# Gather indices of a four-layer graph network: one load of 14 groups into half of a 28-group buffer, in place of one load per group

## What is computed

```python
edge_index = jnp.stack([src, dst])
x = _layernorm(x + _L0_gnn_ref(x, edge_index, edge_weight, ...))   # segment_sum(x[src] * edge_weight, dst)
x = _layernorm(x + _L1_gnn_ref(x, edge_index, edge_attr_64, ...))  # segment_sum(relu(x[src] + edge_attr), dst)
x = _layernorm(x + _L2_gnn_ref(x, edge_index, ...))                # segment_sum(x[src], dst), batch norm
x = _layernorm(x + _L3_gnn_ref(x, edge_index, edge_type_8, ...))   # attention over 8 relations, (x @ W[r])[src]
```

## Time and profile before

| | us |
|---|---|
| median of 3 runs (lowest, highest) | 12603.83 (12548.62, 12606.76) |
| the profiled execution | 12571.97 |
| its span on the core | 12570.2 |
| POOL busy in the span | 6491.1 (52%) |
| PE, DVE, ACT busy | 3621.9 (29%), 3237.4 (26%), 329.6 (3%) |
| pass 0 gathers from, to | 11.4, 2535.4 |
| pass 3 gathers from, to | 8331.9, 10916.5 |

### The profile page before, as it was taken

One profiled execution on the slowest core, in us unless ns is written; L12 is line 12 of the kernel. 1 busy time (PEld: TensorE's weight loads), 2 busy tenths in 40 slices (PEclk: granted clock), 3 DMA queues, 4 the chain that ended last, 5 costly groups with the idle time before them and its releaser, 6 DMA issues.

```text
span 12570.2 us, 99249 instructions
## 1 busy us (share of the span) xinstructions
PE 3621.9 (29%) x17244; PEld 2968.1 (24%) x17245; DVE 3237.4 (26%) x5805; ACT 329.6 (3%) x648; POOL 6491.1 (52%) x6716
## 2 busy tenths in 40 slices
PE   2222222242222222432232223640000000003558
PEld 2222222242222222322222222220000000002555
DVE  2111211141111111221111111322222222286554
ACT  0000000010000000000000000100000000000000
POOL 6666666525556566346666665035555555402443
PEclk6555555555555555555555555555555555556885
DMA  1111111111111111111111111232222222302220
GB/s 41 21 21 21 20 21 21 20 37 40 40 41 41 41 42 41 37 27 22 22 22 22 22 22 23 65 100 64 64 65 65 64 66 66 64 0 48 72 71 19
DMA packets 620736, 509.88 MB, mean 41 GB/s; under 512 B 405721, under 2 KB 405721, under 8 KB 620574
## 3 DMA queue, kind: packets, MB, share of 16 engines
q0 software_dynamic: 200704, 212.34, 9.2%
q1 hardware_dynamic: 391778, 239.40, 7.5%
q10 hardware_dynamic: 28224, 57.82, 1.2%
HBM read 405.06 MB, written 103.99 MB: 40 GB/s over the span
## 4 chain that ended last, share of the span: by engine, by line
another core or an unknown queue 32%; issue 21%; DVE 16%; DVEq 15%; PE 14%; ACT 1%; DMA 1%; POOL 0%; ACTq 0%; POOLq 0%; SPq 0%; PEldq 0%
PE p_sum L679 6%; DVEq L213 5%; DVE oh L931 3%; DVEq L931 2%; DVE oh L945 2%; DVEq L926 1%; DVEq L209 1%; PE p_a L777 1%; DVEq L1193 1%; DVEq L1189 1%; DVE sel L1196 1%; DVE sel L1200 1%; DVE msg L1005 1%; PE p_sum L834 1%
## 5 line engine op out<-in xcount | busy, mean ns | idle before, releaser
L486 POOL DMA_INDIRECT gat<-x_d,idx x3136 | 3034.9, 968 | 2241.3 <-DMA idx<-in_src_p 1272.4
L679 PE MATMUL p_sum<-oh,msg 128*66 128x128 f32 (+1 forms) x6272 | 1410.8, 418 | 3681.1 <-DVE oh L931 1676.8
L486 POOL DMA_INDIRECT gat<-rel_d,idx x1568 | 1492.0, 952 | 1612.6 <-DMA idx<-key_d 1079.3
L679 PEld LDWEIGHTS p_sum<-oh,msg 128*66 128x66 f32 (+1 forms) x6272 | 1269.7, 227 | 3821.7 <-DVE oh L931 2910.5
L486 POOL DMA_INDIRECT gat<-in_x,idx x1568 | 1532.4, 977 | 1001.8 <-DMA idx<-in_src_p 526.5
L937 DVE TENSOR_TENSOR sum_t<-sum_t,p_sum 64x128 f32 (+1 forms) x588 | 165.0, 281 | 5204.9 <-remote 4100.1
L679 PE MATMUL p_sum<-oh,gat 128*64 128x128 f32 x3136 | 687.5, 410 | 1723.1 <-DVE oh L931 1184.6
L679 PEld LDWEIGHTS p_sum<-oh,gat 128*64 128x64 f32 x3136 | 616.6, 219 | 1793.8 <-DVE oh L931 1219.6
L931 DVE SCALAR_TENSOR_TENSOR oh<-dstf,fine_col,iota 128x512 f32<-128x512 f32 x1176 | 835.0, 748 | 510.2 <-issue 406.1
L793 PE MATMUL p_sum<-trip_s,oht 128*128 x2344 | 202.0, 237 | 2410.9 <-DVE oht L1193 1255.6
L793 PEld LDWEIGHTS p_sum<-trip_s,oht 128*128 128x128 bf16 x2344 | 168.8, 166 | 2445.6 <-issue 2445.6
(11 more groups left out here) (240 smaller groups left out, 3061.1 us busy)
## 6 DMA issues: line engine op xcount, KB each, us to landing
he_d<-gat ACTq DMA_DIRECT2D x196, 288.0 KB
gat<-he_d SPq DMA_DIRECT2D x196, 288.0 KB, 2.8
ea<-in_edge_attr SPq DMA_DIRECT2D x196, 256.0 KB
gat<-x_d,idx POOLq DMA_INDIRECT x3136
drow<-dst_d SPq DMA_DIRECT2D x196, 256.0 KB
rel_d<-sum_t SPq DMA_DIRECT2D x14, 2016.0 KB, 6.4
gat<-in_x,idx POOLq DMA_INDIRECT x1568
gat<-rel_d,idx POOLq DMA_INDIRECT x1568
```

Of the source, the lines that this page charges most:

```text
L486: nc.gpsimd.indirect_dma_start(out=gat[:, q, s, 0:width], out_offset=None, in_=table, in_offset=bass.IndirectOffsetOnAxis(ap=idx[:, q, s:s ...
L679: ins = nc.tensor.matmul(p_sum[0:width, 0, 0:W], lhs(q, s), oh[:, 0, s, :], start=(s == 0), stop=(s == S - 1))
```

## The change

The index tile gets IB = 28 places in two halves of 14 groups. One load of 14 groups' indices (128 x 112 int32, 56 KB) takes the place of 14 loads of 4 KB. The four data slots, the 8 gathers per group and all that consumes them stay as they are. Loops of SP and POOL that had 49 turns of 4 groups have IL = 7 turns of 28 groups. POOL waits for `s_idx` once in 14 groups, and for `s_free` at every group as before. SP refills a half when its last four groups' slots are freed; in pass 1 it does so between its `ea` loads, in pass 3 after every 14th `dst_row`.

```diff
+HALF = 14
+IB = 2 * HALF
+IL = G // IB
+PER = IB // Q
...
-        idx = sb("idx", [P, Q, S], i32)
+        idx = sb("idx", [P, IB, S], i32)
...
-            def refill(n, q, it, source):
-
-                wait_reg(sp, s_free[q], it + (2 + IT * n))
-                sp.dma_start(idx[:, q, :], source[:, bass.ds(it * Q + (Q + q), 1), :]
-                             .rearrange("p a s -> p (a s)")).then_inc(s_idx[q], 16)
+            def freed(n, it, i):
+
+                wait_reg(sp, s_free[i % Q], it * PER + (i // Q + 2 + IT * n))
+
+            def refill(n, it, h, source, waited=False):
+
+                last = (h + 1) * HALF - 1
+                for i in range(last - Q + 1, last + 1):
+                    if not waited:
+                        freed(n, it, i)
+                sp.dma_start(idx[:, h * HALF:(h + 1) * HALF, :],
+                             source[:, bass.ds(it * IB + (IB + h * HALF), HALF), :]).then_inc(s_idx[h], 16)
...
             def pass3(it, final):
-                for q in range(Q):
-                    if not (final and q >= Q - 2):
-                        wait_reg(sp, s_drused, it * Q + (q + 1))
-                        dst_row(q % 2, it * Q + (q + 2))
-                    if not final:
-                        refill(3, q, it, key_d)
+                for i in range(IB - 2 if final else IB):
+                    wait_reg(sp, s_drused, it * IB + (i + 1))
+                    dst_row(i % 2, it * IB + (i + 2))
+                    if not final and i % HALF == HALF - 1:
+                        refill(3, it, i // HALF, key_d)
...
             def gather_pass(n, table, width):
-                with pool.Fori(0, IT) as it:
-                    for q in range(Q):
-                        wait_reg(pool, s_idx[q], it * 16 + 16 * (1 + IT * n))
-                        wait_reg(pool, s_free[q], it + (1 + IT * n))
+                with pool.Fori(0, IL) as it:
+                    for i in range(IB):
+                        q = i % Q
+                        if i % HALF == 0:
+                            wait_reg(pool, s_idx[i // HALF], it * 16 + 16 * (1 + IL * n))
+                        wait_reg(pool, s_free[q], it * PER + (i // Q + 1 + IT * n))
                         for s in range(S):
                             nc.gpsimd.indirect_dma_start(
                                 out=gat[:, q, s, 0:width], out_offset=None, in_=table,
-                                in_offset=bass.IndirectOffsetOnAxis(ap=idx[:, q, s:s + 1], axis=0),
+                                in_offset=bass.IndirectOffsetOnAxis(ap=idx[:, i, s:s + 1], axis=0),
```

More of the change, by code:

```diff
@@ L141, in program @@
         s_key, s_keyst, s_zero = sem("s_key"), sem("s_keyst"), sem("s_zero")
-        s_idx = [sem(f"s_idx{q}") for q in range(Q)]
+        s_idx = [sem(f"s_idx{h}") for h in range(2)]
         s_gat = [sem(f"s_gat{q}") for q in range(Q)]
@@ L266, in _ @@
             sp.dma_start(edge_w[:, 0:G, :].rearrange(flat), weight_p.rearrange(flat)).then_inc(s_load[2], 16)
-            for q in range(Q):
-                sp.dma_start(idx[:, q, :], src_p[:, q, :]).then_inc(s_idx[q], 16)
+            for h in range(2):
+                sp.dma_start(idx[:, h * HALF:(h + 1) * HALF, :], src_p[:, h * HALF:(h + 1) * HALF, :])\
+                    .then_inc(s_idx[h], 16)
             sp.dma_start(src_i, src_p.rearrange(flat)).then_inc(s_load[3], 16)
@@ L291, in first_indices @@
                     sp.wait_ge(s_free[q], IT * n + 1)
-                    sp.dma_start(idx[:, q, :], source[:, q, :]).then_inc(s_idx[q], 16)
+                for h in range(2):
+                    sp.dma_start(idx[:, h * HALF:(h + 1) * HALF, :], source[:, h * HALF:(h + 1) * HALF, :])\
+                        .then_inc(s_idx[h], 16)
             def dense_io(n):
@@ L364, in dense_io @@
                 sp.sem_inc(s_table, 1)
-            with sp.Fori(0, IT - 1) as it:
-                for q in range(Q):
-                    refill(0, q, it, src_p)
+            with sp.Fori(0, IL - 1) as it:
+                for h in range(2):
+                    refill(0, it, h, src_p)
             sp.wait_ge(s_keyst, 32)
@@ L377, in _, with pass1 @@
                 sp.dma_start(ea_slot[q], ea_d[q, :, :]).then_inc(s_ea[q], 16)
[L378 to L382, removed]
+            def pass1(it, final):
+                for i in range(IB - Q if final else IB):
+                    freed(1, it, i)
+                    sp.dma_start(ea_slot[i % Q], ea_d[bass.ds(it * IB + (Q + i), 1), :, :]
+                                 .rearrange("a p e -> (a p) e")).then_inc(s_ea[i % Q], 16)
+                    if not final and i % HALF == HALF - 1:
+                        refill(1, it, i // HALF, src_p, waited=True)
+            with sp.Fori(0, IL - 1) as it:
+                pass1(it, False)
+            pass1(IL - 1, True)
             dense_io(1)
             first_indices(2, src_p)
-            with sp.Fori(0, IT - 1) as it:
-                for q in range(Q):
-                    refill(2, q, it, src_p)
+            with sp.Fori(0, IL - 1) as it:
+                for h in range(2):
+                    refill(2, it, h, src_p)
             dense_io(2)
@@ L404, in pass3 @@
             def pass3(it, final):
-                for q in range(Q):
-                    if not (final and q >= Q - 2):
-                        wait_reg(sp, s_drused, it * Q + (q + 1))
-                        dst_row(q % 2, it * Q + (q + 2))
-                    if not final:
-                        refill(3, q, it, key_d)
-            with sp.Fori(0, IT - 1) as it:
+                for i in range(IB - 2 if final else IB):
+                    wait_reg(sp, s_drused, it * IB + (i + 1))
+                    dst_row(i % 2, it * IB + (i + 2))
+                    if not final and i % HALF == HALF - 1:
+                        refill(3, it, i // HALF, key_d)
+            with sp.Fori(0, IL - 1) as it:
                 pass3(it, False)
-            pass3(IT - 1, True)
+            pass3(IL - 1, True)
             sp.wait_ge(s_trip, 2)
```

## The result

| | before | after |
|---|---|---|
| median of 4 runs, us | 12597.92 | 12873.42 |
| lowest, highest | 12548.62, 12606.76 | 12866.36, 12892.37 |
| the profiled execution | 12571.97 | 12866.36 |

What follows compares the result with a forecast made beforehand. Bound: POOL's gathers and its pauses, with long bursts starving DVE. 12,572 - 200 (passes 0 to 2) + 390 (pass 3) + 0 (code) = 12,762, plus 32 for the median: 12,790 us, slower by 1.5%; range 12,180 to 13,140.

Steps and rivals of the forecast that it cites:

- What bounds the kernel: Four gather passes: POOL gathers or waits; a long burst of gathers starves DVE, freed some 4 us after POOL pauses.
- Passes 0 to 2: -200: Index load leaves 189 pauses, 1.9 us each, 360 us if nothing else moves; 200 us saved taken, ends 0 and 360.
- the share that DVE takes back: Passes 0 to 2: DVE loses the free time POOL gains; something over half of 360 us kept as saving, unmeasured.
- The sign to look for: Passes 0 to 2: no POOL wait ends with indices; pauses 2 us shorter in the middle, 7.1 in pass 0.
- Pass 3: +390: Pass 3: index waits no longer brake POOL, bursts of 14 groups starve DVE; 390 us longer, 2,996 us.
- The period of 14 groups: Pass 3: 140 us burst, DVE at rate 0.25 after 13 us, then 67, 4 and 3 us: 214 in place of 186.
- to this come 4 us until DVE moves: Pass 3, each pause after a 14-group burst: DVE moves again 4 us after POOL stops.
- About 13 long waits of 70 us: Sign in pass 3: POOL gathers 140 us without pause, then waits some 70 us for indices, about 13 times, not 61.
- DVE's waits in pass 3: Sign in pass 3: DVE's waits by "remote" and "issue" grow.
- Loops' code: 0: POOL's longer loop body, 28 turns: code fetches of 76 to 306 us possible, taken as zero, hidden in pauses.
- DVE keeps up: Rival, pass 3's 14-group bursts: DVE's rate stays near its average; faster above 0.36, totals 12,018 or 12,442; chance 0.27.
- Another brake: Rival: ACT's sequencer gives slots back late, POOL pauses as before; no change, 12,604 within 60; chance 0.13.

Runs made afterwards that it cites:

- e3: Changed kernel plus a wait: in pass 3 POOL starts a group only when DVE has finished the group two before; 12235.05 us, ratio 0.9734 to the kernel before.
- e1: Changed kernel with the old index loads, order and loops of 4 groups in pass 3 only; 12290.65 us, ratio 0.9768 to the kernel before.
- e7: Changed kernel, but in pass 3 POOL waits before each group until DVE has finished the group six before; 10522.49 us, ratio 1.0002 to the kernel before.
- e10: Repeat of e7 (POOL at most six groups ahead in pass 3) on a third chip; 10511.34 us, ratio 1.0002 to the kernel before.
- e12: Kernel before, with loads of 14 groups in pass 3 only, POOL waiting there for DVE's group six before; 10509.63 us, ratio 1.0003.
- e5: Changed kernel, but in pass 3 POOL waits for DVE before every 7th group, gathering in blocks of 7; 10528.40 us, ratio 1.0006 to the kernel before.
- e11: Repeat of e8 (8 of 72 values a row gathered in pass 3) on a third chip; 10508.83 us, ratio 1.0003 to the kernel before.
- e4: As e3, with the same two-group rule for POOL in passes 0 to 2 too; 12233.06 us, ratio 0.973 to the kernel before.
- e9: Repeat of e5 (POOL gathering in blocks of 7 groups in pass 3) on a third chip; 10513.05 us, ratio 1.0006 to the kernel before.
- e8: Changed kernel, but pass 3's gathers fetch 8 values of each row in place of 72; 10523.70 us, ratio 1.0005 to the kernel before.

## Why the prediction was right

Direction and size came out: 12,790 forecast, 12,873 measured, inside the range. Part of the nearness is luck: passes 0 to 2 saved some 50 us more than forecast and pass 3 lost 154 more, and the two errors partly cancel. Point by point:

- **What bounds the kernel.** Right for this chip. That bursts of gathers starve DVE was read from pass 1's start and from pieces of 0.7 us; e3 bears it out with one wait. What the forecast couldn't see is that another chip doesn't have it at all.
- **Passes 0 to 2: -200.** Measured -250.8 in the traces and -293 by e1, in which pass 3 contributes some 55 (2,604 to 2,549). The 1.9 us a pause were right (8.5 to 6.6 in pass 0; POOL's pauses in the middle went from 8.7 to 6.7, 9.6 to 7.6 and 7.1 to 5.0 us in passes 0, 1 and 2). Mis-sized was the share that DVE takes back: the text took nearly half of 360 us, and it was 109, under a third. By passes, from first to last gather, it came back unevenly: 102, 60 and 91 us saved, where 62, 67 and 60 pauses of 1.9 us would be 118, 127 and 114. The sign to look for, 7.1 us in the middle in pass 0, came out at 6.7.
- **Pass 3: +390.** Right mechanism, too small: +544. The period of 14 groups was put at 214 us and is 3,148.1 / 14 = 224.9. Its terms, from the pause shown: the burst 140, as said; DVE's rate in the slow stretch about 0.22 (20.9 windows in 14 groups, less 12 in the pause and 3 in the first 13 us, leave 5.9 of 5.37 us in some 143 us), between the 0.21 of the row and the 0.25 taken; load and restart 3.2 against 3; the time until DVE moves 16 against 4. That last term failed: "to this come 4 us until DVE moves" was read behind bursts of 30 to 40 us. In the eleven long pauses, behind bursts of 140 us, DVE's slow pieces go on for 12 to 17 us, 16 in the mean. That is 12 more than taken, eleven times: 132 of the 152 us by which 3,148 is over the 2,996 forecast. POOL's waits for slots, most of them in the first 28 groups, which the sum didn't have, are another 34; the other terms cancel to within 15.
- **About 13 long waits of 70 us.** 12 inside the pass: one of 39.4 and eleven of 83.8 in the mean. The first 28 groups are loaded ahead, and POOL has no wait for indices in them. The text spoke of 14 equal periods; the count is one less, and the work that the missing pause doesn't hold comes at the end, where DVE goes on for 189 us after the last gather (19 before). Of the other sign, DVE's waits in pass 3, half came out: those ended by "issue" grew from 966 to 1,681 us, those by "remote" shrank from 584 to 268.
- **Loops' code: 0.** Right. A turn of POOL's loop has 264 instructions in the changed kernel (the forecast took about 275), and the packets rose from 21 to 30, far below one for each of 28 turns. The loop of pass 3 with a wait at each group (e3, e7, e10, e12) has 320, and that is loaded again. In e7, over one turn of 280 us (queue of code loads: packets, MB, share):

```profile
q14 instruction: 5, 0.04, 0.0%
```

By the Trainium skill (Runtime: NRT & Kernel Launch, Instruction fetch mechanics) a taken branch to code outside the two blocks of 256 instructions that are held stalls the engine until it is fetched. No such stall shows: in e5 to e12, where POOL has no pauses to hide one, no two gathers of a pass have more than 0.32 us between them, at the turns as elsewhere. The kernels with loops of 28 groups there take 1 to 10 us more than the kernel before (e5 to e11), where the least that the forecast gave for such loads was 76. On the first chip e3, with 60 packets, and e4, with 92, are the fastest kernels.
- **The rivals.** *DVE keeps up* needed a rate above 0.36 and fell on the first chip at 0.22; on the other three DVE does keep up, at a rate near 1. There the rival would have been right about DVE and wrong about the gain: with DVE at full pace the index loads had no pause to shorten. *Another brake* was there for a short time: ACT's sequencer is slowed too (some 70 instructions of 0.6 to 0.8 us in the kernel before, 880 in the changed one), and in the first 28 groups POOL stands still for slots that ACT frees, four times, 25.8 us in all. The profile names ACT for 7.0 of them and puts the rest to "remote". In the eleven bursts behind them no slot is late by more than 2 us.

What stays open. Whether the length of a burst alone sets the loss, or the distance between POOL and DVE, isn't told apart by e3, which shortens both: the runs made for it fell on chips that don't show the effect. The trace of the changed kernel speaks for the gathers in progress: in each long pause POOL has gathered at least 14 groups more than DVE has used, and DVE runs at full pace (12 windows in 62 us behind 9038.10). That a far look-ahead without long bursts costs nothing is not shown. Whether bytes or the issuing of the gathers starve the sequencers is open for the same reason; against the bytes speaks that the hold goes on when next to none move (32 packets from 9021 to 9036), and that in pass 3 of e12 more bytes move per us (86 GB/s against 54) without it. The changed kernel itself wasn't run on the other chips; the runs that stand for it there are that kernel with one more wait, which never holds POOL up (e5 to e7, e9, e10), or with 8 values a row (e8, e11). And nothing here says why one chip has the starvation and three haven't: different series ran on different chips, so a passing state of the first isn't excluded, though two series, with the kernel before at 12,598 and 12,584, showed the same. The chip of the first of these two series isn't on record; "the first chip" is that of e1 to e4.

The version to keep is e3: 2.7% faster than the kernel before, and 5% than the changed one, where the starvation exists. Where it doesn't, its relatives with other start values (e5 to e7) cost at most 10 us (0.1%); e3 itself wasn't run there. e1, with the old pass 3, can't be told from e3: their intervals overlap.

## What to carry to other kernels

A buffer that frees a fast producer from its consumer also takes away the pauses in which the consumer had the machine to itself; before decoupling, look at what the consumer does while the producer runs, and if it is slow then, keep the producer a fixed small number of steps ahead. When a recovery time is read behind short bursts with good pauses between them, don't carry it over to bursts four times as long. And look at how long sequencer instructions take (DVE's take 0.045 us in the middle, and 0.7 where they are held) before a time is put down to the program: the same kernel took some 12,590 us on one chip and 10,510 on three others, and edits worth 2% to 5% on the first moved nothing on the others.

## What was not expected of the hardware

- On the chip of e1 to e4, and in the first series, DVE's sequencer, and ACT's too, takes 0.7 us for an instruction, with 0.7 us between them. In pass 3 it begins in the middle 11 to 14 us into a row of indirect transfers from POOL that follows a pause of over 5 us, in passes 0 to 2 mostly 14 to 20. SP's is slowed as well (some 500 such instructions in the kernel before, 40 in the changed one), PE's hardly (9 and none). The hold outlasts POOL's last gather: up to 5 us behind bursts of 30 to 40 us in the old pass 3, 12 to 17 us behind bursts of 140 us, and 10 us once behind a burst of 31 us that followed others closely, though the gathered data has landed.
- On three other chips there is none of it, in rows of gathers of 2,000 us without a pause. The kernel before is 16% faster on them; the traces of e5 to e12 there have nearly the same busy times as those of the first chip.
- The kernels there agree within some 0.2% (10,506 to 10,528 us) whatever is done to the index loads; POOL's 1.25 to 1.30 us per gather is then the bound of all four passes.
- A loop of POOL of 264 instructions isn't loaded again at its turns, one of 320 is (5 packets, 40 KB a turn), and the loads cost POOL nothing that the trace shows.
